# Later inverse scales moved to ScalarE and GpSimd, gates earlier in the drain, and a last stage of five steps with head weights stationary and maxima in the mask's first row

## What is computed

```python
# quantised network: per token scale of the first product, three bf16 parts of its inverse are
# needed because the bias is added inside the scaled product
scale = 127.0 / clip(max(abs(h)), 1e-5)          # h = layernorm(x), one number a token

# mLSTM attention, per head (8 heads of width 32), q = layernorm(x), k = v = context
log_fg = log_sigmoid(f_pre); lf = cumsum(log_fg)             # gates: q, k, v times ifgate_w
log_d = lf[t] - lf[s] + i_pre[s], -inf where s > t
m = max(log_d, over s)                                       # 128 tokens x 8 heads a batch
s_mat = (q k' / sqrt(32)) * exp(log_d - m)
denom = maximum(abs(sum(s_mat)), exp(-m)) + 5e-5
y = (s_mat v) / denom        # then a norm over each head, a gain, and x = x + y

# last layer: xn = layernorm(x); gates = softmax(xn gate_w); x = x + xn W + sum_e gate_e V_e U_e xn
```

## Time and profile before

| | us |
|---|---|
| three executions | 388.62, 390.67, 391.48 (median 390.67) |
| profiled execution | 389.47 |
| its span in the trace | 387.8 |
| TensorE busy with products | 335.4 (86%) |
| VectorE, ScalarE, GpSimd busy | 292.0, 285.5, 238.6 |
| mean granted TensorE clock | 0.974 of full speed |

### The profile page before, as it was taken

How to read it: one execution, slowest core, us unless ns; L and a number is a source line. 1 busy time by engine, 2 the same in 40 slices (tenths; PEclk the granted TensorE clock), 3 DMA queues, 4 the chain that set the end, 5 groups by cost and what they waited for, 6 DMA issues and landing times.

```text
span 387.8 us, 9058 instructions
## 1 busy us (share of the span) xinstructions
PE 335.4 (86%) x2948; PEld 226.6 (58%) x2955; DVE 292.0 (75%) x1018; ACT 285.5 (74%) x600; POOL 238.6 (62%) x289
## 2 busy tenths in 40 slices
PE   7999689999999998677829999877877999999976
PEld 6777556667676664333425565555455666666654
DVE  3998755777988997879888778784246887787884
ACT  6656585587677768766848999977667888888843
POOL 2114734878798887499976999971005556446460
PEclk9999999999999999996869999989999999999999
DMA  7999989979574600000000000000001122212101
GB/s 235 306 285 257 272 248 251 235 220 240 128 154 93 110 3 3 1 0 0 2 0 1 3 0 2 1 2 0 2 14 30 30 42 56 56 35 51 41 15 55
DMA packets 44141, 33.67 MB, mean 87 GB/s; under 512 B 19904, under 2 KB 40256, under 8 KB 43968
## 3 DMA queue, kind: packets, MB, share of 16 engines
q1 hardware_dynamic: 44096, 33.11, 33.8%
HBM read 24.71 MB, written 8.39 MB: 85 GB/s over the span
## 4 chain that ended last, share of the span: by engine, by line
PE 60%; DVE 13%; ACT 12%; issue 9%; POOL 5%; DVEq 0%; POOLq 0%; ACTq 0%
PE PS L1456 5%; PE PS L1672 5%; PE PS L1812 4%; PE PS L1574 4%; PE PS L1804 4%; ACT h2T L1284 4%; PE PS L1698 3%; PE PS L1629 3%; PE PS L1540 3%; PE PS L1526 2%; PE PS L1774 2%; PE PS L1549 2%; PE PS L1797 2%; PE PS L1557 2%; PE PS L1679 2%
## 5 line engine op out<-in xcount | busy, mean ns | idle before, releaser
L689 DVE TENSOR_REDUCE negm<-PS 128x4 bf16<-128x512 f32 x64 | 40.9, 684 | 12.5 <-PE PS L1549 12.4
L1211 ACT ACTIVATE pT<-PS 128x512 f32<-128x512 f32 x64 | 36.4, 595 | 17.1 <-PE PS L1540 16.3
L515 POOL TENSOR_TENSOR kst<-kst,rows 128x1024 f32<-128x1024 f32 x16 | 37.9, 2366 | 10.1 <-ACT kst L1277 9.9
L1353 ACT ACTIVATE lnT<-PS,Atok 128x128 f32<-128x128 f32 x128 | 36.3, 368 | 2.0 <-DVE lnb L965 0.8
L532 POOL TENSOR_TENSOR kst<-kst,rows 128x1024 f32<-128x1024 f32 x14 | 33.0, 2359 | 0.0
L554 POOL TENSOR_TENSOR smd<-smd,mhalf 128x1 f32<-128x1 f32 x16 | 9.0, 562 | 37.1 <-DVE smd L1033 37.1
L1574 PE MATMUL PS<-pT,vx 128*32 128x128 f32 x512 | 27.3, 285 | 2.1 <-ACT pT L1211 2.1
L1672 PE MATMUL PS<-w2q,h2T 128*128 128x256 bf16 x128 | 20.1, 310 | 9.0 <-ACT h2T L1284 9.0
L560 POOL TENSOR_TENSOR rr<-ms,mhalf 128x8 f32<-128x8 f32 x16 | 26.3, 1643 | 1.9 <-DVE ms L1047 1.9
L965 DVE SCALAR_TENSOR_TENSOR lnb<-PS,lnT 128x512 f32<-128x512 f32 x32 | 20.6, 683 | 8.0 <-PE PS L1774 5.8
L1812 PE MATMUL PS<-wd,xT 128*128 128x392 f32 (+2 forms) x80 | 25.3, 441 | 0.8 <-ACT xT L1376 0.7
(11 more groups left out here) (260 smaller groups left out, 1028.8 us busy)
## 6 DMA issues: line engine op xcount, KB each, us to landing
scr_q<-qpart SPq DMA_DIRECT2D x8, 384.0 KB, 3.2
scr_k<-kpart SPq DMA_DIRECT2D x8, 384.0 KB, 4.2
X<-in_x SPq DMA_DIRECT2D x8, 256.0 KB, 4.9
CTXT<-in_ctxT SPq DMA_DIRECT2D x8, 256.0 KB, 5.2
vx<-in_ctx SPq DMA_DIRECT2D x16, 128.0 KB, 2.7
out<-rest SPq DMA_DIRECT2D x16, 128.0 KB, 1.7
rows<-in_rows SPq DMA_DIRECT2D x1, 1544.0 KB, 8.0
qst<-scr_q SPq DMA_DIRECT2D x8, 192.0 KB, 4.5
```

What stands on the lines that cost most here:

```text
L515: gp.tensor_tensor(n2[q.slot], n2[q.slot], ln2g, ALU.mult).then_inc(b_g2, 1)
L689: v.tensor_reduce(negm[f.slot % 2][:, 4 * hg:4 * hg + 4], PS[:, 2 + hg % 2, :].rearrange("p (h k) -> p h k", h=4), AX_X, ALU.max, negate=T ...
L1211: s.activation(pT[:, hg, :], PS[:, hg % 2, :], ACT.Exp, scale=float(DH0) ** -0.5).then_inc(a_e, 1)
L1353: last = s.activation(dT[half][:, cols], PS[:, half, cols], ACT.Exp, scale=1.0, bias=Atok[:, n.b, h:h + 1])
```

## The change

1. *Inverse scales of batches 8 to 15.* The product with the weight mean goes to ScalarE (`up_scales`), VectorE keeps one reciprocal for each four batches (`inverses`), and GpSimd cuts them into parts (`later_parts`), in turns 2 and 8. `columns` of batch 12 waits for the second set.
2. *Drain of the quantised network.* When no new batch enters, TensorE does `gates(g)` first in its turn instead of behind the down product.
3. *The last stage.* `values` now has a head's 128 columns of weights stationary and streams its 33 value columns (32 and the ones), so the result already has tokens down the partitions; `back` and `value_columns` are gone, and so is a step: five steps instead of six, with `scores` in step `n`. The maxima, in one bf16 part, are sent by a transfer from `Mb` into row 0 of a mask that is stored once for each of 32 heads' slots (`masks`), and `log_d` is one 512-column product with `onerow` (the identity with a first row of ones). What the rounding leaves of a maximum goes into the denominator by `EM` and `EF`. GpSimd fills `masks` by four copies in turns 0 to 3 of the first attention. VectorE's `norms` is taken apart: `row_stats(c)`, `denominators(a)`, `finish(d)`, `mean_squares(a)`, then `weights(n)` at the end of the turn. `keep_busy` products are added in turns 0 to 2 and in the tail, and the drain is rewritten for four batches.

The core of the diff:

```diff
 # SyncE
+            def load_maxima(b):
+                done(sp, c_arg, Turn(b, 0, 0), -3, 2)
+                sp.dma_start(masks[0:1, b % 4 * H1:(b % 4 + 1) * H1, :],
+                             Mb[b * H1:(b + 1) * H1, :]).then_inc(m_ld[b % 4], 16)
...
+            sp.wait_ge(g_m, 1)
+            sp.dma_start(masks[0:1, :, :], Mb[0:4 * H1, :]).then_inc(m_first, 16)
...
 # GpSimd
+            def later_parts(i):
+                some = slice(8 + 4 * i, 12 + 4 * i)
+                pool.wait_ge(b_i, 8 + i)
+                for k in range(3):
+                    step(gp.tensor_copy(ivp[:, some, k], iv[:, some]))
+                    if k < 2:
+                        step(gp.tensor_tensor(iv[:, some], iv[:, some], ivp[:, some, k], ALU.subtract))
+                gp.tensor_copy(ivp[:, some, 3:5], ivp[:, some, 0:2]).then_inc(b_ip, 1)
+                gp.tensor_copy(ivp[:, some, 5], ivp[:, some, 0]).then_inc(b_ip, 1)
...
 # VectorE
+            def inverses(i):
+                dve.wait_ge(s_sr, 3 + i)
+                v.reciprocal(iv[:, 8 + 4 * i:12 + 4 * i], uw[:, 8 + 4 * i:12 + 4 * i]).then_inc(b_i, 1)
                 elif tau == 7:
-                    inverse_parts(8, NB)
+                    inverses(1)
             def turn_cd(n, a, c, _e, d):
                 if d:
                     gate_max(d)
                     gated(d)
-                if a:
-                    weights(a, 0)
-                    weights(a, 1)
                 if c:
                     heads(c)
+                    new_rows(c)
+                    row_stats(c)
+                if a:
+                    denominators(a)
                 if d:
                     finish(d)
-                if c:
-                    new_rows(c)
-                norms(b, c)
+                if a:
+                    mean_squares(a)
+                if n:
+                    weights(n, 0)
+                    weights(n, 1)
...
 # ScalarE
+            def up_scales(i):
+                some = slice(8 + 4 * i, 12 + 4 * i)
+                act.wait_ge(l_c, l_links(12 + 4 * i))
+                act.wait_ge(s_wq, 1)
+                s.activation(uw[:, some], unit1[:, some], ACT.Copy, scale=wmean[:, 0:1]).then_inc(s_sr, 1)
             def turn_cd(n, a, c, e, d):
                 if d:
                     gate_exp(d)
-                if b:
-                    head_values(b)
                 if e:
                     row_columns(e)
+                if n:
+                    exp(n, 0)
                 if d:
                     gated_columns(d)
-                if n:
-                    exp(n, 0)
                 if a:
-                    value_columns(a)
+                    head_values(a)
                 if n:
                     exp(n, 1)
...
 # TensorE
             def turn_b(a, _b, _p, _q, c, d, _e, f, g):
                 if a and a.b > 2:
                     columns(a)
+                if g and not a:
+                    gates(g)
...
             def log_d(n, half):
-                t.matmul(bank, identb[:], maskb[:].unsqueeze(1).to_broadcast([128, 4, 128]), start=True, stop=False)
-                for j in range(4):
-                    last = t.matmul(bank[:, j * 128:(j + 1) * 128], rowsel[:, hs + j:hs + j + 1].to_broadcast([128, 128]),
-                                    MPARTS[:, n.used, :], start=False, stop=(j == 3))
+                last = t.matmul(PS[:, half, :], onerow[:], masks[:, hs:hs + 4, :], start=True, stop=True)
             def values(a):
                 for h in range(H1):
-                    last = t.matmul(PS[64 * (h % 2):64 * (h % 2) + 64, 6, (h // 2) * 128:(h // 2 + 1) * 128],
-                                    vx2[a.slot % 2][:, h, :], smT[h // 4][:, (h % 4) * 128:(h % 4 + 1) * 128],
-                                    start=True, stop=True)
+                    last = t.matmul(PS[:, 6, 64 * h:64 * h + DH1 + 1], smT[h // 4][:, (h % 4) * 128:(h % 4 + 1) * 128],
+                                    vx2[a.slot % 2][:, h, 0:DH1 + 1], start=True, stop=True)
             def turn_cd(n, a, _c, e, d):
                 if e:
                     turn_rows(e)
+                if n:
+                    log_d(n, 0)
+                if a:
+                    values(a)
                 if d:
                     turn_gated(d)
                 if n:
-                    log_d(n, 0)
+                    log_d(n, 1)
+                    if n.b < 3:
+                        keep_busy(7, 6)
                 if d:
                     expert(d)
-                if a:
-                    values(a)
                 if n:
-                    log_d(n, 1)
-                    if n.b == NB - 1:
-                        scores(n)
+                    scores(n)
                 if e:
                     wide_all(e)
```

365 lines of the change are left out of this document (154 added, 211 removed).

## The result

The changed kernel takes 394.36 us (median of 4 executions, 394.09 to 396.73) beside 390.59 us for the kernel before: a ratio of 1.0117, 95% interval 1.0062 to 1.0172 (the ratio is that of the means; the quotient of the two medians is 1.0097). A later job gave 396.49 beside 390.74, ratio 1.0139 (1.011 to 1.0168). Both intervals lie above 1, and the loss is under 2%. The forecast was 388.0, a gain of 2.7; the median lies within its range of 383.5 to 395.5, but the time moved the other way. The profiled execution took 396.73 us with a span of 395.0. It was the slowest of its kernel and the profiled one of before was among the quickest, so the two spans differ by 7.2 us, more than the medians do. The ledger is made over those 7.2.

A forecast was written before the change was run, and what follows sets the result against it. GpSimd was taken to bound the quantised network and TensorE the last stage, VectorE 10% behind. Terms -4.4 - 1.3 + 2.2 + 3.7 - 2.9 = -2.7 gave 388.0 us against the 390.67 median; 8-in-10 range 383.5 to 395.5.

The forecast's parts named there:

- The inverse scales: Quantised network: GpSimd's two idle stretches, 5.9 us, go and seven small steps cost 1.5; -4.4 us.
- rival 4: Quantised network: GpSimd's small casts wait for VectorE instead, and the drain gains nothing; 391.7 us, chance 12%.
- The drain: End of the quantised network: gates done first fall under ScalarE's copy; -1.3 us, ends 0 and -2.5.
- The start of the last stage: First mask product to fourth values: transfer, added `keep_busy` and longer value products cost +2.2 us, from +1 to +3.5.
- The transfer: Ahead of the last stage's first mask product: sending the maxima replaces six small steps; 0 to +1 us.
- The full turns: Last stage, values of batch 3 to batch 15: 12 turns of 5.94 us, +3.7, ends -1 and +8.
- The ring: Full turn of the last stage: a chain of waits through all engines sets its length, 5.94 us.
- The tail: Last values to the end: less turning back, one root fewer, four batches drained; -2.9 us, from -1.5 to -4.
- Rival 1: Last stage quicker: VectorE's 5.7 us a turn alone bounds, and the start is 0.7 shorter; 384.4 us, chance 20%.
- Rival 2: Last stage's value products: each costs weight load plus stream, 0.135 us; +7.2, so 395 us, chance 15%.
- Rival 3: Last stage: TensorE's clock halves in four of twelve full turns; +10, so 398 us, chance 8%.
- a granted clock below full after 290 us: Sign in the last stage's profile that the forecast, and the time with it, is wrong.

The follow-up runs named there:

- the kernel in both places: Changed kernel, its six `keep_busy` products in turns 0 to 2 kept, four more added ahead of the values in turns 1 to 3: 391.34 us, ratio 1.0037.
- the gates back: Changed kernel with the quantised network's gates returned behind the down product in all turns: 392.89 us, ratio 1.0087.
- scales and masks: Kernel before plus the new inverse scales and, of the new last stage, only the mask products: 386.18 us, ratio 0.9874.
- both places and the gates back: Changed kernel plus four `keep_busy` products ahead of the values in turns 1 to 3, gates again behind the down product: 390.32 us, ratio 0.9997.
- scales + gates: Kernel before plus the new inverse scales and the gates first in the drain, old last stage: 385.70 us, ratio 0.9873.
- the 64 columns: Changed kernel with value products over all 64 columns of a head's tile instead of 33: 394.97 us, ratio 1.009.
- scales, masks and `keep_busy`: Kernel before plus inverse scales, new mask products and five `keep_busy` products per turn of the last stage's start (two in turn 0): 383.69 us, ratio 0.9824.
- one part alone: Kernel before plus only the new inverse scales on ScalarE, VectorE and GpSimd: 384.21 us beside 391.06, ratio 0.984.

## Why the prediction was wrong, point by point

- **The inverse scales: right, a little short.** Forecast -4.4, measured -5.3 between profiled executions. The small steps cost 1.63 us (forecast 1.5), and neither rival 4 nor a wait in their place came. What was missed are the small delays that followed the bubble.
- **The drain: no gain.** Forecast -1.3. Measured, with one pair of profiles each, -0.3 and -0.1 up to the last transposed gates, which is within the scatter, and +1.2 to +1.3 in the passage for the clock that is halved there. The term had only the work on TensorE's path in it and not the clock.
- **The start of the last stage: the step that failed.** Forecast +2.2, measured +10.5. Two assumptions in it were wrong: the size of `keep_busy`, and the clock. "The added `keep_busy` products put the first scores, then the first values, some 0.6 us later": they stand on the path of the scores three times, for 1.29, 2.56 and 2.53 us. And the whole term was made at full clock, which is the larger part. By the kernel in both places, which had 1.00, the new start costs 16.4 us at full speed, 2.6 more than the old; the other 5.7 of its 8.4 us are the clock. That is an estimate, since this kernel has four more products in each turn. In the passage 1.2 to 1.3 of the 2.1 are the clock (12.54 against 11.22 with the gates back). So of 10.5 us some 7 are the clock, and 3.5 the term that I had put at 2.2. The transfer, put at 0 to +1 there, is about +0.3 in the kernel with scales and masks.
- **The full turns: right in kind, a little long.** Forecast 5.94 a turn, measured 5.80; +2.6 instead of +3.7. The ring was put 0.14 too high and lies just above VectorE's own loop, put at "nearly 5.8" and measured at 5.75. Twelve turns of 5.80 would be +2.0; the other 0.5 is the first of them, 6.31 us, at whose beginning the clock was still down.
- **The tail:** -1.8 instead of -2.9, within the ends given. Its terms, and the `keep_busy` products in it, were not tried alone.
- **Ahead of the network:** +1.7, forecast 0. That varies whatever the setup: the kernel with both places and the gates back, which has the new mask setup too, starts its first long multiplication at 163.88, as the kernel before does at 163.74, while scales + gates, with the old setup, starts it at 165.45. A dip of the clock in slice 6, as here, goes with a late start in nine profiles (165.1 to 165.8), and four of the five without it start at 164.3 or before. The kernel in both places has no dip and starts at 165.19, so the dip is not the whole cause, which stays open.
- **Rival 1** (quicker last stage) did not come. **Rival 2** (loads that don't hide) is refuted by the 64 columns: 0.113 us a product against 0.111. The rule it stood on, in the Trainium skill, "TensorE: Matmul & The Clock Gate", Part 3, says that loads overlap products in flight only where row groups differ; all of these products use all rows, so here the measurement decides against that rule.
- **Rival 3** (the clock falls in the last stage) is what happened, at 8%. It had the mechanism, and its 398 is 3.6 above the median, but the place was wrong: I put the half speed into the full turns, which stayed at 1.00, and not into the start, where TensorE has scores, masks, thin values and `keep_busy`, and waits in between. The quoted sign, "a granted clock below full after 290 us", was the right one to watch. That the median fell into the range all the same is luck: its upper part was there for rival 2.

What stays open is the exact condition. Denser starts kept the clock in two pairs of kernels, but executions of one kernel differ, and no run here separates more streaming from less idling: every product that was added did both, and the values over 64 columns, which only stream more, scatter too widely (391.6 to 396.3). Before each fall in the changed start TensorE idled: in its three full-speed parts (283.5 to 287.6, 291.1 to 294.5, 297.9 to 301.3) it was busy for 7.7 of 10.9 us. In the starts that kept the clock it was busy for 11.03 of 13.80 (before), 11.71 of 13.80 (scales, masks and `keep_busy`) and 15.37 of 16.41 us (both places).

## What to carry to other kernels

A change that makes TensorE's work cheaper should be read for the clock as well: in pipeline fills and drains, where fewer products overlap, less work on TensorE can halve the speed of all that is left, weight loads too. Whether the clock is held must be looked at over the whole kernel: in both profiled kernels with `keep_busy` in both places it stayed up in the start and fell later, in the tail (0.91 and 0.89). Placeholder products belong into stretches where the engine waits anyway; on the path they cost their time and, where the clock falls in spite of them, twice their time. And when several gains come in one change, build each alone: here one part alone was worth 6.9 us by the medians (5.3 between the profiled executions), and the rest gave back more.

## What was not expected of the hardware

- The clock fell three times in a start in which TensorE's longest wait was 1.15 us. The busy share misleads here: by its records TensorE was busy for 91% of it (20.14 of 22.16 us), but that share is made by the half speed, which stretches every product; in the full-speed parts ahead of the falls it is 71%. The Trainium skill, "TensorE: Matmul & The Clock Gate", in "Why this matters for your kernels", blames idle gaps between bursts of products for such drops. The trace agrees in so far as each fall stands behind waits, but no single one was long, and a wait of 0.93 us ahead of the values of the kernel before, with 0.76 twice behind it, brought no fall.
- A load of 128 float32 columns hides the stream of 33 and of 64 columns alike (1.78 and 1.81 us for sixteen), and takes twice as long at half clock (3.54 us).
- With nothing but added products that nobody reads, the start of a stage got 2.4 us shorter (16.21 to 13.80).
